# Perceiver stack on one Trainium2 core: the score products of the first cross attention issued as four column tiles of 32 keys each

## The reference, cut to what matters

```
x = x + _L0_xattn_ref(_layernorm(x), ctx_768, mask, Wq, Wk, Wv, Wo)
    q = (x @ Wq).reshape(B, N, 16, 16)          # B = 4, N = 256
    k = (context @ Wk).reshape(B, M, 16, 16)    # M = 4096
    v = (context @ Wv).reshape(B, M, 16, 16)
    attn = softmax(where(mask, einsum('bhid,bhjd->bhij', q, k) / 4, max_neg))
    out = einsum('bhij,bhjd->bhid', attn, v) @ Wo
```

## Time and profile before

| what | us |
|---|---|
| median of 3 runs | 2125.9 (2125.27 to 2126.0) |
| the profiled execution, its own time | 2122.2 |
| its span in the trace | 2120.4 |
| TensorE busy in it | 1764.8 |
| VectorE busy | 1222.5 |
| ScalarE busy | 1020.4 |
| GpSimd busy | 762.8 |

### The profile page before, as it was taken

How to read it: one execution, slowest core, us unless ns; L and a number is a source line. 1 busy time by engine, 2 the same in 40 slices (tenths; PEclk the granted TensorE clock), 3 DMA queues, 4 the chain that set the end, 5 groups by cost and what they waited for, 6 DMA issues and landing times.

```text
span 2120.4 us, 34682 instructions
## 1 busy us (share of the span) xinstructions
PE 1764.8 (83%) x13676; PEld 1119.4 (53%) x13676; DVE 1222.5 (58%) x2979; ACT 1020.4 (48%) x1381; POOL 762.8 (36%) x669
## 2 busy tenths in 40 slices
PE   4969998999899998888788859678686658987885
PEld 2535554465456555565577425445453456676663
DVE  5142423423242401546676589899999977447776
ACT  1448667757766894222221345565564621214552
POOL 6343425433441410000120048687797840110000
PEclk7979999999999998999887656788786769999987
DMA  6657555674756452000100002132131152000000
GB/s 148 124 115 132 121 121 105 131 136 107 131 117 134 83 118 79 1 1 2 38 16 2 13 8 75 46 98 83 53 90 46 53 204 76 1 1 1 1 6 15
DMA packets 78045, 150.01 MB, mean 71 GB/s; under 512 B 15464, under 2 KB 63144, under 8 KB 71464
## 3 DMA queue, kind: packets, MB, share of 16 engines
q1 hardware_dynamic: 64304, 101.80, 16.9%
q0 software_dynamic: 12768, 42.59, 13.0%
q10 hardware_dynamic: 792, 3.17, 0.4%
HBM read 93.59 MB, written 2.62 MB: 45 GB/s over the span
## 4 chain that ended last, share of the span: by engine, by line
PE 58%; DVE 25%; POOL 6%; DMA 4%; issue 3%; ACT 3%; DVEq 0%; ACTq 0%; POOLq 0%
PE R L112 35%; PE B L112 21%; DVE CA L1685 5%; DVE PM L1730 5%; PE B L178 2%; POOL KST L790 2%; DMA KST<-OV 2%; POOL ACC L1811 2%; DVE CA L1697 1%; DVE T L1699 1%; ACT PM L1615 1%; ACT PS L2369 1%; DVE MX L2525 1%; DMA CN<-in_ctxn 1%; POOL LNrs L200 1%
## 5 line engine op out<-in xcount | busy, mean ns | idle before, releaser
L571 ACT ACTIVATE P<-R 128x1024 f32<-128x1024 f32 x512 | 500.9, 1029 | 167.0 <-PE R L112 151.3
L112 PE MATMUL R<-QS,KST 100*128 100x256 bf16 x2048 | 273.0, 277 | 28.9 <-ACT RT L116 16.7
L112 PE MATMUL B<-P,VP 128*32 128x256 f32 x4096 | 278.6, 389 | 3.3 <-issue 2.9
L112 PEld LDWEIGHTS R<-QS,KST 100*128 100x128 bf16 x2048 | 182.7, 99 | 156.3 <-issue 67.5
L1811 POOL TENSOR_TENSOR ACC<-ACC,PM 128x4096 f32<-128x4096 f32 x22 | 195.1, 8870 | 1.8
L200 POOL TENSOR_TENSOR LNrs<-LNve,pk_const 128x2 f32<-128x2 f32 x36 | 25.4, 704 | 443.6 <-DVE LNve L196 443.2
L112 PE MATMUL R<-OV,QT 32*128 32x512 f32 x512 | 182.9, 801 | 0.0
L790 POOL DMA_DIRECT2D KST<-OV x300 | 145.1, 492 | 68.6 <-PE R L112 55.9
L112 PEld LDWEIGHTS B<-P,VP 128*32 128x32 f32 x4096 | 107.8, 110 | 105.2 <-issue 35.2
L601 DVE CAST OV<-RT 128x512 bf16<-128x512 f32 x64 | 27.0, 423 | 183.3 <-ACT RT L116 110.8
L1801 POOL TENSOR_TENSOR SM<-SM,NG 128x1 f32<-128x1 f32 x30 | 79.3, 2643 | 144.1 <-DVE PM L1730 144.1
(11 more groups left out here) (345 smaller groups left out, 3432.6 us busy)
## 6 DMA issues: line engine op xcount, KB each, us to landing
KST<-OV POOLq DMA_DIRECT2D x276, 128.0 KB, 10.7
CT<-in_ctxP SPq DMA_DIRECT2D x40, 768.0 KB, 4.7
CN<-in_ctxn SPq DMA_DIRECT2D x60, 384.0 KB, 3.4
CT<-in_ctxT SPq DMA_DIRECT2D x64, 192.0 KB, 2.5
KST<-OV SPq DMA_DIRECT2D x84, 128.0 KB, 9.7
KST<-in_ctxP ACTq DMA_DIRECT2D x4, 768.0 KB, 9.4
QS<-x_q POOLq DMA_DIRECT2D x24, 128.0 KB, 5.3
pk_a<-in_pk_a SPq DMA_DIRECT2D x1, 3014.0 KB, 10.1
```

The costliest lines, as they stand in the source:

```text
L112: return e.matmul(o, l, r, start=st, stop=sp, skip_group_check=True)
L571: e.activation(P[(32 * p + k0) % 3][:, :], ring.at(("s", p, k0))[:, :], ACT.Exp).then_inc(*EX.up((p, k0)))
```

## The change

Each score product of 128 keys becomes four products of 32 keys. Product j takes 32 of the keys and writes PSUM partitions 32j to 32j + 31, so it lies in column tile j of the array, the tiles in which the weighted values lie. The moving operand, the result and its place are the same, and the semaphore is raised once, by the last of the 16.

```
                     for hh in range(4):
-                        ins = mm(e, ps[:, hh * 256:hh * 256 + 256], KST[buf][0:100, hh, kt * 128:kt * 128 + 128],
-                                 QS[b % 2][0:100, 4 * g + hh, :], True, True)
+                        for j in range(4):
+                            ks = slice(kt * 128 + 32 * j, kt * 128 + 32 * j + 32)
+                            ins = mm(e, ps[32 * j:32 * j + 32, hh * 256:hh * 256 + 256], KST[buf][0:100, hh, ks], QS[b % 2][0:100, 4 * g + hh, :], True, True)
                     ins.then_inc(*QK.up((p, kt)))
```

## The result

The changed kernel takes 2199.37 us (median of 4 runs, 2191.55 to 2203.62) against 2125.95 us of the kernel before on the same chip: 1.0335 times as long, 95% interval 1.0299 to 1.0372, or 73 us more. The profiled execution took 2202.36 us, its span is 2200.5. The change starts at line 498 and adds a line, so from there on a line of before has one number more (the exponential L571 is L572, the refill L790 is L791).

The account below looks back on a forecast made before the run. TensorE bounds plain pairs of key tiles, ScalarE only 0.17 us behind. Terms -29 + 56.4 + 6.9 = +34 us on the profiled 2122.2 give 2156.5; the median, 3.7 above, is 2160 us, range 2088 to 2208.

Parts of the forecast that it names:

- TensorE's busy time and what waits take of it: Score stage: fewer tiling switches shorten plain pairs from 1.98 to 1.81 us, 29 us off after waits absorb some.
- stops by issue beyond those already there: During the 15 refills of KST, TensorE runs out of instructions: 59.3 us, less 2.9 already there, 56.4 added.
- half clock behind the stops: After each of five long stops, TensorE runs a pair at half clock: 6.9 us added in all.
- The gain: Score stage: four score products 0.107 us apart, a pair 1.71 us on TensorE, 1.81 by ScalarE; 29 us off.
- The covers: Three buffers each of R and P; if ScalarE falls behind, the score run needing its buffer is late next.
- 21.7 - 5.5 - 9.5 + 2.2 = 8.9 us: Refill beside plain pairs: packetless stretch, less earlier request served, less instructions held, plus restart; costs 8.9 us.
- The stock of 503 instructions: TensorE holds about 503 instructions, a bit over two packets; they last 9.5 us in new plain pairs, 21 before.
- 4.5 us of waiting for the refill itself: Groups 2: in two of three refills this waiting absorbs some of the stop, leaving 4.4 us each.
- the 1.37 us: Pair behind a stop of 5 us took 3.35 instead of 1.98 us; 1.37 counted for each of five stops.
- Packets come in time: Rival: during refills packets come within about 6 us of being asked for, only the 29 us count; 2097 us, chance 0.30.
- The half pace (0.214): Rival: bfloat16 column tiles in the scores run at 0.214 us a group, a pair takes 2.57; 2250 us, chance 0.06.
- the four in series: Rival: the four score products don't run side by side, 2.5 us more in each of 256 pairs; 2770 us, chance 0.02.

## Why the prediction was right in its direction and too small by half

The mechanism, the direction and the sign of each term were as forecast. The size was not: +73 us on the median where +34 stood. Step by step, on the 81 us of the stage:

| term | forecast, us | measured, us |
|---|---|---|
| TensorE's busy time and what waits take of it | -29 | -36.0 busy, +3.7 in the query waits |
| stops by issue beyond those already there | +56.4 | +95.0, of which 8.3 only replace waits for the key copy |
| half clock behind the stops | +6.9 | +27.0 |
| sum | +34 | +81 |

*The gain* was right. Score groups came 0.109 us apart (0.107 taken from float32 records of the next stage), the pair takes 1.74 on TensorE (1.71) and 1.83 where ScalarE binds (1.81). The covers stood: the R and P buffers are named in 0.6 and 0.5 us of waiting. The query waits grew by 3.7 as TensorE arrives earlier.

*The stops* are the step that failed, and it is the working "21.7 - 5.5 - 9.5 + 2.2 = 8.9 us" a refill with the counts behind it. By kind of block (the gaps by issue in order of time, summed):

| refill in | forecast, us | measured, us |
|---|---|---|
| groups 0 of batches 1 to 3 | 18.3 | 12.2, of which 2.0 at the branch of "max" |
| groups 3 | 10.8 | 15.6 |
| groups 1 | 7.5 | 6.2 |
| groups 2 | 17.7 | 39.5 |
| blocks 13 and 14 | 5 | 17.0 |
| block 0 | 0 | 7.9, of which its wait for the key copy gives back 7.0 |

Two things were wrong in it. First, I took a refill as one stretch without packets, with one stop at its end. The stock of 503 instructions was right: in block 10 the last packet before the refill comes at 610.4, and TensorE runs dry at 620.1, 9.7 us later (9.5). The first stop alone, 7.4 us, is even less than the 8.9. But the packet that ends it brings 256 instructions, the next one is again 13 us away (624.2 to 637.1), and a second stop of 5.3 us follows, which the working has no term for. The length that I had measured, about 21 us, was the wrong one to build on: it also held the slow consumption of before, when at 24 instructions a microsecond a packet lasted TensorE 10 us, so that half of the silence was time in which it needed none. The record fits that: in block 10 the packet under the refill came 22.0 us after the one before it in the kernel before (559.9 to 581.9), 13.8 us in the changed one (610.4 to 624.2). No run separates the two parts. What sizes the loss is the time from one packet to the next under a refill: around the twelve stops over 5 us it is 12 to 18 us, with a median near 15 (22 where a query wait lies in it). The refill of block 10 lasts 29 us, and a block that uses a packet in 4.6 us stops behind each: 11.5, 15.1 and 12.7 us in the three groups 2, not 8.9, and 5.2 in the mean of groups 3, not 3.6. In block 10 from 611.2 to 640.0 TensorE ran 705 instructions, 12.8 us of work at 55 a microsecond; it lost 16 of 28.8 us. Second, I set "4.5 us of waiting for the refill itself" against the stops of groups 2, and 5 us for blocks 13 and 14 without any working. But what TensorE itself had waited there was short (0.97 us in the earlier trace rows, 1.3 in all), and those waits are gone now; little was absorbed. Blocks 13 and 14 hold plain pairs like groups 2, and by my own 8.9 they should have had 17.8; 17.0 were measured. In groups 0, in turn, the stops were shorter than I had reckoned, perhaps because the value, tail and output products gave the packets more time.

*The clock.* One pair at half pace behind five stops was too little on both counts. There are twelve stops over 5 us. And the 1.37 us were read from one pair, while the half clock of the earlier trace rows had begun before it, with the query transposes at 346.76. That stretch of the kernel before, and then block 10 of the changed one (stretches: us, busy us of PE, PEld, DVE, ACT, POOL, clock, DMA share, GB/s):

```profile
346.70:351.00 4.30, 4.24 (x28) 2.50 (x28) 1.67 (x6) 1.31 (x2) 0.00 (x0) 0.55 0.96 120
```

```profile
627.50:631.70 4.20, 4.20 (x65) 3.00 (x68) 0.00 (x0) 1.59 (x2) 0.00 (x0) 0.50 1.07 184
...
640.00:645.00 5.00, 5.00 (x80) 3.71 (x83) 0.00 (x0) 2.55 (x3) 0.00 (x0) 0.50 0.01 3
```

4.2 and at least 5.0 us at a granted clock of 0.50 (1.2 GHz of 2.4), half of which is lost: over 2 us a stop, where the stretch of before had already lost 1.9 (4.3 us at 0.55).

*The rivals.* "Packets come in time" fell: under a burst they don't, one comes in 13 us. Its condition, a packet within about 6 us of being asked for, can't be read directly, since the trace doesn't show when a fetch is asked for. With the refills small it is what happens, but for block 0, and 25 of the 29 us of gain that it promised are there. The half pace (0.214) and the four in series fell by 0.109. What "Runtime: NRT & Kernel Launch", section Instruction fetch mechanics, of the Trainium skill says (the next page is fetched beside the current one, mostly hidden) holds here without a refill, in block 15, and not under one, where nearly all of the 98.4 us stand. By the turns between queues packet by packet, which the Trainium skill has in "DMA: Bandwidth & Descriptors", section Queues, rings and completion order, one would look for a fetch earlier than 13 us, whatever the backlog. The trace doesn't agree: with the backlog small, four came in 26 us, with a burst one. Why is open, and no run here looked at the single DMA engines.

## What to carry to other kernels

Count the instructions of the engine that bounds, not only its time: compare its instructions per microsecond with packets of 256 that arrive one in 13 us behind a burst of 24 copies of 128 KB, and about one in 7 where the copies are issued one or two at a time. Lay denser code where the DMA engines are idle, or issue the copies in small portions, and look in the trace whether they really go out so. To size such a stall, look for what depends least on the kernel's own pace (here the time from packet to packet under load), not for the length of a silence that the old pace helped to make. And a stop of 5 us or more cost another 2 us at half clock behind it here.

## What the runs showed of the hardware

- Four bfloat16 products of 32 keys and 256 queries in the four column tiles cost what one product of 128 keys does: 0.109 us for either. Staying in the same tiling between scores and weighted values saves 0.24 us a pair on TensorE (1.98 to 1.74, two changes a pair); cut into 64-key tiles it saves nothing (2.00).
- Instruction fetches: one packet in 13 us behind a burst of 24 copies of 128 KB on the 16 DMA engines (a share of 1.03 over 26 us), four in 26 us where the copies were issued one or two at a time, at the same share (1.01). 98.4 us of stops at 96 instructions a pair, 20 to 22 at 64, 3.4 at 48.
- A refill spread over the block behind other work on GpSimd's queue came out as 8 to 18 DMAs at once in the odd blocks, and the stops fell by only a fifth in all (98.4 to 76.8 us), but by half in the even blocks, where it was spread (61.9 to 31.4).
- GpSimd's 18 DMA issues ahead of a layer norm had cost TensorE 5.1 us in each of three blocks. With the layer norm behind the first of them those waits are gone, and the whole kernel takes 0.9927 of its time.
